# Token halves as slot groups, and expert rows gathered back by token, in a fused mixture-of-experts and attention kernel

## The reference

```
x = x + 0.5 * moe_ffn(layernorm(x))
x = x + attention(layernorm(x))        # 16 heads of 16, rope on q and k, causal softmax
x = x + 0.5 * moe_ffn(layernorm(x))

moe_ffn(x): probs = softmax(x @ gate_w.T)             # 8 experts
            top_w, sel = top_k(probs, 2); top_w /= sum(top_w)
            per expert e: (silu(x @ w_gate[e]) * (x @ w_up[e])) @ w_down[e]     # F = 176
            weighted sum of the two chosen experts' outputs
```

## Time and profile before

| | us |
|---|---|
| median of 3 runs (1216.02 to 1219.74) | 1216.24 |
| the profiled execution's own time | 1216.84 |
| its span, first to last instruction | 1215.1 |
| busy PE, DVE, ACT, POOL | 1002.9, 846.8, 630.8, 588.9 |

### The profile page before, as it was taken

The page is one execution under the profiler, slowest core; times in us unless marked ns, Lnnn a source line. Parts: engine busy times, 40 slices in busy tenths (PEclk is TensorE's granted clock), DMA queues, the critical chain, the costliest instruction groups (busy, mean ns, idle before and its releaser), DMA issues. The chain is left out here.

```text
span 1215.1 us, 24056 instructions
## 1 busy us (share of the span) xinstructions
PE 1002.9 (83%) x6998; PEld 644.2 (53%) x6998; DVE 846.8 (70%) x2632; ACT 630.8 (52%) x1318; POOL 588.9 (48%) x756
## 2 busy tenths in 40 slices
PE   1649998974888489999999999999988569998850
PEld 1438997863767223333333333333347349998750
DVE  5585444435999498999989998988529684443347
ACT  1504554444777216666666666666774505554430
POOL 2937777765999302222222222222239127777740
PEclk9857999996999659999999999999989858999985
DMA  6803333325565511111111111110022413333349
GB/s 212 278 12 102 105 102 104 105 92 158 155 180 164 161 61 47 57 56 60 59 57 57 56 60 55 55 54 2 2 75 71 140 31 105 104 103 104 104 149 338
DMA packets 84524, 121.19 MB, mean 100 GB/s; under 512 B 10920, under 2 KB 63920, under 8 KB 81200
## 3 DMA queue, kind: packets, MB, share of 16 engines
q1 hardware_dynamic: 63424, 75.08, 19.8%
q0 software_dynamic: 13632, 37.24, 9.7%
q10 hardware_dynamic: 7344, 7.34, 1.8%
HBM read 75.51 MB, written 43.78 MB: 98 GB/s over the span
## 5 line engine op out<-in xcount | busy, mean ns | idle before, releaser
L1352 ACT ACTIVATE a_probs<-a_ps_s 128x1024 f32<-128x1024 f32 (+3 forms) x384 | 294.2, 813 | 172.8 <-PE a_ps_s L1384 171.6
L1267 POOL TENSOR_SCALAR_AFFINE_SELECT a_probs<-a_probs 128x256 f32<-128x256 f32 x256 | 102.9, 408 | 368.9 <-ACT a_probs L1352 366.2
L1285 DVE CUSTOM_DVE_ANT_0 a_unused<-a_ps_m,const_sb 128x128 bf16<-128x128 f32 (+3 forms) x512 | 234.1, 485 | 26.6 <-PE a_ps_m L1369 16.7
L1369 PE MATMUL a_ps_m<-st_k,st_q 96*128 96x512 bf16 (+3 forms) x768 | 219.6, 344 | 22.3 <-PEq L167 14.9
L378 POOL DMA_INDIRECT v_sb<-xn_dram,f_token_i x142 | 139.7, 984 | 104.7 <-DVE f_token_i L486 62.0
L1287 DVE TENSOR_REDUCE a_max_a<-a_ps_m 128x1 f32<-128x512 f32 x256 | 175.7, 686 | 13.9 <-PE a_ps_m L1369 13.7
L1384 PE MATMUL a_ps_s<-st_q,st_k 98*128 98x512 bf16 (+3 forms) x768 | 180.6, 329 | 1.5 <-ACT a_probs L1352 1.4
L532 DVE TENSOR_TENSOR f_h<-f_ps_gu,f_sg 128x176 f32<-128x176 f32 x142 | 48.5, 341 | 185.2 <-ACT f_sg L598 185.1
L1369 PEld LDWEIGHTS a_ps_m<-st_k,st_q 96*128 96x128 bf16 x768 | 67.8, 98 | 194.3 <-DVE a_max_a L1287 55.2
L1397 PE MATMUL a_ps_ctx<-a_probs,a_v_st 128*32 128x512 f32 (+3 forms) x1536 | 163.6, 498 | 1.3 <-POOL a_probs L1267 0.7
L382 POOL DMA_INDIRECT y_dram<-v_sb,f_pair_i x142 | 140.0, 986 | 44.0 <-issue 38.1
(11 more groups left out here) (193 smaller groups left out, 2018.8 us busy)
## 6 DMA issues: line engine op xcount, KB each, us to landing
xn_dram<-v_sb SPq DMA_DIRECT2D x64, 128.0 KB, 3.7
v_sb<-y_dram SPq DMA_DIRECT2D x32, 256.0 KB, 5.5
st_q<-qk_dram SPq DMA_DIRECT2D x16, 384.0 KB
st_k<-qk_dram SPq DMA_DIRECT2D x16, 384.0 KB
st_q<-y_dram SPq DMA_DIRECT2D x16, 256.0 KB, 3.3
st_k<-y_dram SPq DMA_DIRECT2D x16, 256.0 KB, 3.2
qk_dram<-st_rT_hi SPq DMA_DIRECT2D x16, 256.0 KB, 3.0
qk_dram<-st_rT_mid SPq DMA_DIRECT2D x16, 256.0 KB, 3.5
```

The source lines that it names most:

```text
L1267: pool.affine_select(out=tri, in_=tri, compare_op=ALU.is_ge, fill=zero, base=0, pattern=[[0, 2], [1, P]], channel_multiplier=-1).then_inc( ...
L1285: dve.tensor_tensor_reduce(unused[:, bank, 0:nk], ps, cst("mask")[:, HALF - nk:HALF], 1.0, NEG, ALU.add, ALU.max, at).then_inc(taken, 1)
L1352: act.activation(probs[:, s % 4, :, 0:nq], ps_s[s % 2][:, :, 0:nq], ACT.Exp, scale=float(HD) ** -0.5).then_inc(exp_done, 1)
L1369: pe.matmul(ps_m[bank][:, 0:nk], q_st[b][0:MAX_ROW, h, P * i:P * i + P], k_st[b][0:MAX_ROW, h, k0:k0 + nk], start=True, stop=True).then_in ...
```

## The change

Slots are grouped by token half first and by expert within it: the first 39 slot tiles (CT = 32 + 7) hold pairs of the first 16 token tiles only, the other 39 those of the last 16. That makes 78 slot tiles instead of 71. One scan over 256 values takes the place of eight, with a correction at the edge of each of 16 groups (edge, shift). Owners are found in three passes over (slot tiles, lots): (0 to 16, lots 0 and 2), (16 to 39, lots 0 and 2), (39 to 78, lots 1 and 3), 96 matmuls instead of 128; pair_i and the treatment of empty slots are gone.

The results are no longer scattered. SP stores each slot tile linearly to y_dram, and GpSimd gathers 128 rows of 1 KB back by token, one indirect transfer for each token tile and choice (gather_y, with the rows' numbers kept in y_rows). The 32 gathers of the first half run beside the experts of the second half, one a step from step 43 on, and VectorE mixes them into x_sb three steps behind (mix); in f1 VectorE takes the statistics of these 16 tiles in the same steps and GpSimd raises the 16 variances to the power at the end, in f2 SP issues four of the eight output stores in these steps. The 32 gathers of the second half come behind the experts: in f2 right away, in f1 within the projection (four gathers in five steps, GATHERS), where ScalarE now weighs both results and GpSimd adds both; VectorE's mix_second is gone. The sum of the rope's two products moves from GpSimd to VectorE for the first 22 tiles (LATE) and stays on GpSimd for the last ten.

```diff
-SLOT_TILES = TOPK * NT + E - 1
+HALVES = 2
+HT = NT // HALVES
+CT = TOPK * HT + E - 1
+SLOT_TILES = HALVES * CT
+ROWS_OF_HALF = TOPK * HT
...
+YB = 8
+Y_LAG = 4
+MIX_LAG = 3
...
+def token_row(m):
+
+    return 2 * (m // 4) + m % 2, m // 2 % 2
+
+
+def rows_mixed(t):
+
+    return 4 * (t // 2) + t % 2 + 3
...
+        OUT_AT = [CT + Y_LAG + MIX_LAG + 8 * (q + 1) - 1 for q in range(HT // 4 - 1)] + [SLOT_TILES - 1]
+
+        def store_out(eng, q):
+
+            eng.wait_ge(mixed, 8 * (q + 1))
+            eng.dma_start(out[q * 4 * P:(q + 1) * 4 * P, :].rearrange("(t p) d -> p t d", p=P), x_sb[:, 4 * q:4 * q + 4, :]).then_inc(out_stored, 16)
...
+            for j in range(SLOT_TILES):
+                sp.wait_ge(y_out, j + 1)
+                sp.dma_start(y_dram[j * P:(j + 1) * P, :], y_sb[:, j % DEEP, :]).then_inc(stored[j % DEEP], 16)
+                if out is not None and j in OUT_AT:
+                    store_out(sp, OUT_AT.index(j))
             for q in range(DEEP):
-                sp.wait_ge(scattered[q], 16 * len(range(q, SLOT_TILES, DEEP)))
+                sp.wait_ge(stored[q], 16 * len(range(q, SLOT_TILES, DEEP)))
             if out is not None:
-                for t in range(NT):
-                    sp.wait_ge(mixed, t - 7 + 8)
-                    sp.dma_start(yb[:, t % 8, :, :].rearrange("p c d -> p (c d)"),
-                                 y_dram[t * P * TOPK:(t + 1) * P * TOPK, :].rearrange("(p c) d -> p (c d)", c=TOPK)
-                                 ).then_inc(y_in[t % 8], 16)
...
-            def scatter(j, slot, pair):
-                pool.wait_ge(y_out, j + 1)
-                pool.indirect_dma_start(y_dram, bass.IndirectOffsetOnAxis(ap=pair, axis=0), y_sb[:, slot, :], None).then_inc(scattered[slot], 16)
-
-            def step(j, u, token, pair):
-
-                if token is not None:
-                    if j + XDEEP + 1 == FIRST:
-                        pool.wait_ge(slots_ready, 2)
+            def gather_y(m):
+                t, c = token_row(m)
+                wait(pool, mixed, m - YB + 1)
+                row = y_rows[:, c * NT + t:c * NT + t + 1]
+                pool.indirect_dma_start(yg[:, m % YB, :], None, y_dram[0:CT * P, :] if m < ROWS_OF_HALF else y_dram, bass.IndirectOffsetOnAxis(ap=row, axis=0)).then_inc(y_in[m % YB], 16)
+
+            def wait_stored(tiles):
+                for q in range(DEEP):
+                    pool.wait_ge(stored[q], 16 * len(range(q, tiles, DEEP)))
+
+            for j in range(-XDEEP - 1, SLOT_TILES + 2):
+                ahead = j + XDEEP + 1
+                if is_tile(ahead):
+                    if ahead in (FIRST, CT):
+                        pool.wait_ge(slots_ready, 2 if ahead == FIRST else 3)
                     wait(pool, xT_ready, j + 2)
-                    gather((j + XDEEP + 1) % XDEEP, token)
-                if pair is not None:
-                    scatter(j - 2, (j - 2) % DEEP, pair)
-
-            def fixed_step(j):
-                step(j, j % 4, token_i[:, j + XDEEP + 1:j + XDEEP + 2] if is_tile(j + XDEEP + 1) else None, pair_i[:, j - 2:j - 1] if is_tile(j - 2) else None)
-
-            for j in range(-XDEEP - 1, SLOT_TILES + 2):
-                fixed_step(j)
+                    gather(ahead % XDEEP, token_i[:, ahead:ahead + 1])
+                if j == CT + Y_LAG:
+                    wait_stored(CT)
+                if 0 <= j - CT - Y_LAG < ROWS_OF_HALF:
+                    gather_y(j - CT - Y_LAG)
+            if out is not None:
+                wait_stored(SLOT_TILES)
+                for m in range(ROWS_OF_HALF, TOPK * NT):
+                    gather_y(m)
+            else:
+                norm = Own(pool, norm_own)
+                norm.then_wait(pool.memset(minus_half[:], -0.5))
+                pool.wait_ge(var_ready, HT // 4)
+                norm.then_wait(pool.tensor_tensor(rstd[:, 0:HT], rstd[:, 0:HT], minus_half[:], ALU.pow))
+                norm.then_wait(pool.tensor_tensor(nmr[:, 0:HT], nmr[:, 0:HT], rstd[:, 0:HT], ALU.mult))
...
+            by_group = [P, GROUPS, HT]
+            base_by_group = base[:].rearrange("p (g t) -> p g t", t=HT)
...
+            for half in range(HALVES):
+                of = slice(E * half, E * (half + 1))
+                own.inc(dve.tensor_tensor_scan(last_tile[:, of], ones_bf[:, 0:E], n_tiles[:, of], float(CT * half), ALU.mult, ALU.add))
             own.wait()
...
-            def tile_hits(at, lot, j0, j1, ready):
-
-                n, of = j1 - j0, slice(LOT * lot, LOT * (lot + 1))
+            def row_hits(lot):
+
+                own.inc(dve.tensor_tensor(at_row[:, lot, :, :], count_lot[:], slot_p[:, LOT * lot:LOT * (lot + 1)].unsqueeze(1).to_broadcast([P, P, LOT]),
+                                          ALU.is_equal))
+
+            def tile_hits(i, lot):
+
+                j0, j1, lots = PASSES[i]
+                at, n, of = at_tile[i][:, lots.index(lot), :, :], j1 - j0, slice(LOT * lot, LOT * (lot + 1))
                 hit, by_tile_no, per_tile = at[:, n:2 * n, :], at[:, 0:n, :], [P, n, LOT]
                 own.then_wait(dve.tensor_tensor(hit, count_lot[:, j0:j1, :], slot_j[:, of].unsqueeze(1).to_broadcast(per_tile), ALU.is_equal))
-                own.then_wait(dve.tensor_tensor(by_tile_no, hit, tile256[:, of].unsqueeze(1).to_broadcast(per_tile), ALU.mult))
-                dve.tensor_scalar(hit, hit, cst("low")[:, LOT * lot // NT:LOT * lot // NT + 1], None, ALU.mult).then_inc(ready, 1)
...
+                own.then_wait(dve.tensor_tensor(by_tile_no, hit, tile128[:, of].unsqueeze(1).to_broadcast(per_tile), ALU.mult))
+                dve.tensor_scalar(hit, hit, cst("low"), None, ALU.mult).then_inc(one_hot_ready, 1)
+
+            def owners(i):
+
+                j0, j1, _ = PASSES[i]
+                ps, n, of = ps_owner[i], j1 - j0, slice(j0, j1)
+                dve.wait_ge(owned, i + 1)
+                own.then_wait(dve.tensor_scalar(low[:, of], ps[:, n:2 * n], -1.0, None, ALU.add))
+                own.then_wait(dve.tensor_tensor(token_up[:, of], ps[:, 0:n], low[:, of], ALU.add))
+                dve.tensor_scalar(token_i[:, of], token_up[:, of], T - 1, None, ALU.bitwise_and).then_inc(slots_ready, 1)
+
+            for lot in LOTS_OF[0]:
+                row_hits(lot)
+                tile_hits(0, lot)
+            for lot in LOTS_OF[0]:
+                tile_hits(1, lot)
+            owners(0)
+            for lot in LOTS_OF[1]:
+                row_hits(lot)
+                tile_hits(2, lot)
...
-            later_hits(2)
-            later_hits(3)
+            owners(1)
...
-            dve.wait_ge(later_owned, 1)
-            owners(ps_later, FIRST, SLOT_TILES)
+            owners(2)
...
+            def mix(m):
+                t, c = token_row(m)
+                dve.wait_ge(y_in[m % YB], 16 * (m // YB + 1))
+                if c:
+                    dve.wait_ge(mixed, m - 1)
+                dve.scalar_tensor_tensor(x_sb[:, t, :], yg[:, m % YB, :], w_mix[:, c, t:t + 1], x_sb[:, t, :], ALU.mult, ALU.add).then_inc(mixed, 1)
+
+            moments_of = Moments(dve, stats_own, stats, mv, x_sb, rstd, nmr)
+
+            def moments_after(m):
+
+                for t in range(HT):
+                    if rows_mixed(t) + 1 == m:
+                        dve.wait_ge(mixed, rows_mixed(t))
+                        moments_of.tile(t, t % 8)
+                    if rows_mixed(t) + 2 == m and t % 4 == 3:
+                        moments_of.four(t // 4, var_ready)
...
+                if 0 <= j - CT - Y_LAG - MIX_LAG < ROWS_OF_HALF:
+                    mix(j - CT - Y_LAG - MIX_LAG)
+                if out is None:
+                    moments_after(j - CT - Y_LAG - MIX_LAG)
...
-            def mix(t, u, c):
-                dve.scalar_tensor_tensor(x_sb[:, t, :], yb[:, u, c, :], w_mix[:, c, bass.ds(t, 1)], x_sb[:, t, :],
-                                         ALU.mult, ALU.add).then_inc(mixed if c else mix_own, 1)
...
             if out is not None:
-                for t in range(NT):
-                    mix_step(t, t % 8)
-                dve.wait_ge(mix_own, NT)
-                mix(NT - 1, 7, 1)
+                for m in range(ROWS_OF_HALF, TOPK * NT):
+                    mix(m)
+            else:
+                for m in range(SLOT_TILES + 2 - CT - Y_LAG - MIX_LAG, ROWS_OF_HALF + 4):
+                    moments_after(m)
...
-                wait(act, scattered[u], 16 * (j // DEEP))
+                wait(act, stored[u], 16 * (j // DEEP))
...
-            for i in range(TOPK * NT):
-                lot = i // LOT
-                pe.wait_ge(first_hot_ready, lot + 1)
-                mm = pe.matmul(ps_first, at_row[:, lot, :, i % LOT], at_first[:, lot, :, i % LOT], start=(i == 0), stop=(i == TOPK * NT - 1))
-            mm.then_inc(first_owned, 1)
-            for i in range(TOPK * NT):
-                lot = i // LOT
-                pe.wait_ge(later_hot_ready, lot + 1)
```

(76 more changed lines are left out.)

213 lines of the change are left out of this document (98 added, 115 removed).

## The result

The changed kernel took 1238.99 us (median of 4 runs, 1235.87 to 1241.44) where the kernel before, measured beside it, took 1216.77 (1216.02 to 1219.74). The ratio is 1.0177, interval 1.0146 to 1.0207: 1.8% slower. I had forecast 1211.6, with a range from 1206 to 1223.

What follows compares the result with a forecast made beforehand. Bounds by stage: VectorE in routing, TensorE then GpSimd in experts, VectorE and GpSimd in projection. Through hand-over -4.0, projection -5.8, tail +5.2: -4.6 from 1216.84 gives 1212.2, less 0.6 is 1211.6 us; range 1206 to 1223.

Steps and rivals of the forecast that it cites:

- Routing: In each FFN, up to the first gate_up: VectorE's shorter list lets gate_up of tile 0 start 5.9 us earlier.
- Experts: Both FFNs: TensorE's 2.13 us a tile holds for all 78 tiles; last y_copy at 264.0 (f1) and 1169.3 (f2).
- rival D: Experts: first-half gathers not hidden, GpSimd falls behind and VectorE waits for y rows; +10, 1222 us; chance 0.10.
- Tail: Second FFN, last y_copy to the end: store landing, 31 gather periods, landing, mix, end; 50.95 us, +5.2 in the sum.
- Rival B: Tail and projection: each gather is held by a mix, locked in step; at a 1.50 us period 1224.2 us; chance 0.11.
- G: Period of one GpSimd row gather in projection and tail, taken as 1.30 us; 0.63 us in all for each 0.01.
- 4.0 of barrier: First FFN's hand-over: after about 3.4 us behind y_copy, a barrier of 4.0 us, so the projection starts at 271.4.
- I price a sum at 1.0: Projection: each of 22 rope sums moved to VectorE costs 1.0 us, leaving its list level with GpSimd's.
- what ends is GpSimd's list: Projection: GpSimd's work up to tile 22's rope sum sets the path; tile 24's rope at +97.7, was +103.5; -5.8 us.
- Rival C: Projection: VectorE's rope sums take 1.4 us, its list 9 us longer than GpSimd's; 1220.6 us in all; chance 0.11.
- Rival A: Projection and tail: nothing contends, gather period 1.27 us, rope sums 0.69 us; 1206.7 us in all; chance 0.14.
- the 2.6 us that I took for a row gather: Landing time of a row gather, put at 2.6 us in experts and tail.

Runs made afterwards that it cites:

- run of the second FFN alone: The kernel before with the changed FFN in its second place only, first FFN and projection as before: 1223.59 us, ratio 1.0048.
- early drain: The changed kernel with one GpSimd drain added behind the last row gather of the first FFN's first half: 1228.09 us, ratio 1.0087.
- distance run: The changed kernel with gathered rows in the projection weighed four steps behind their gather instead of two, added five instead of three: 1233.25 us, ratio 1.0118.
- run with all mends: The changed kernel with early drain, rope sums reading PSUM, rows weighed and added two steps later, and a drain ahead of f2's tail: 1210.12 us, ratio 0.9928.

## Why the prediction failed, step by step

**Routing** was right twice: -6.1 and -5.8 for -5.9. **Experts** were right to 1.1 us (f1) and 0.2 (f2); rival D, the first half not hidden, is excluded. Its sign, VectorE waiting for y rows inside the experts, is there (6.6 us in f1, 6.9 in f2), but in the steps from 43 to 60 TensorE's tiles are 2.13 and 2.16 us apart. **Tail**: 50.48 for 50.95, by nearly the same terms (2.8 for the store, 31 x 1.25, 2.8 for the last landing, 0.5 for the mix, 5.6 to the end). Rival B, the lockstep with the mix, is excluded there: G is 1.25. The run of the second FFN alone shows that its +5 stands by itself.

**Hand-over: the step "4.0 of barrier" failed.** The 3.4 ahead of it was right (264.91 to 268.11 is 3.2). The 4.01 of the earlier trace rows is the price of a barrier behind a stage in which GpSimd had issued no indirect transfer. Behind f1 its drain ran 9.04 us. In the kernel before the same drain ran beside the landing of the last scatters and ended 3.2 us behind it, and I priced that whole stretch as a landing. So I took away a wait that wasn't the last one; I had not asked what else stood in those 8.7 us. What follows GpSimd's last work is 10.9 us (9.24 of drain, 1.66 to the first instruction) where I had put 4.0. The early drain shows it: 5.39 instead of 14.10.

**Projection: the step "I price a sum at 1.0" failed**, and with it the path, "what ends is GpSimd's list". The mean over all 22 sums is 1.62. At 0.62 more each, 22 sums are 13.6 us on VectorE, and it is VectorE that tile 24 hangs on: GpSimd's sums of tiles 22 and 23 wait for VectorE's products (1.57 and 1.10 us), the other way round than I had it. GpSimd's list grew by less: G is 1.34 over all 32 gathers (1.16 busy, 0.18 issue) for the forecast 1.30, and not the 1.40 and more behind rival B, since the first nine run ahead of the first sum; an add is 0.86 for 0.76. That is some 4 us together. Beside the held sums VectorE stands idle for 12.7 us between 340 and tile 24, 9.3 of them in the two waits behind late rows shown above. By these numbers the two are more than the 19.8 us that tile 24 is late (+117.5 for +97.7), so at 1.0 a sum VectorE's list was some 6 us shorter than GpSimd's and not level with it; that is an estimate from the terms named here. The evidence was in the rows that I quoted: VectorE's mix at 0.76 instead of 0.44, that is, held for part of each GpSimd instruction. I used it to weigh G and not for the new sum, which reads SBUF twice just as the mix did. And I bounded the sum by one GpSimd add; it can be caught by r_low (1.16) or by two instructions in a row (2.44 at 334.93). The base was off as well: 1.08 at the least, where I took the 0.69 of the earlier trace rows. That row is a product that writes its result in plain order; the rope sum writes its result with a step of four elements. Whether this is the reason, no run shows. Rival C, a sum of 1.4, was right in kind, with a chance of 0.11. It gave 1220.6 and fell short because it left GpSimd at full pace, and knew nothing of the drain and the late rows. Rival A, nothing contends, is excluded by the same rows.

The Trainium skill, SBUF — State Buffer, section "SBUF: two separate sides", calls the interface that VectorE and GpSimd share an exclusive lock, held for the whole instruction, which a VectorE instruction with two SBUF inputs contends for with a GpSimd instruction that reads SBUF. The trace agrees: 0.96 and 0.95 from r_low's end to the sum's end in the timeline above, 0.71 twice from the sum's end to the gather's. Which part of a gather is held, no run here shows. The same page of the Trainium skill, section "Who interferes with whom", says that a VectorE instruction with at most one SBUF input stays out of it, the performance modes aside; 1.10 for 1.63 with one operand in PSUM agrees.

**Landing: the 2.6 us that I took for a row gather** held in the tail (2.8) and not in the projection (up to 10.2 beside SyncE's loads). The distance of two steps between gather and weighing was not examined as a wait at all, though the prediction did so for the three steps in the experts: what was queued behind it was x_high, and with it the next tile. The distance run is worth 0.59%, some 7 us.

**How the miss adds up.** The hand-over's 6.7 is the drain. Of the projection's 21.3, the run with all mends gives back 20.0 (157.59 to 137.63), against 136.3 forecast: with the three costs gone the number that I had summed is right to 1.3 us. In part that is luck. It is one profile of each, the length of one projection is uncertain by about 6 us, and the path is another than I summed: from tile 0's rope to tile 24's VectorE is busy 81.5 of 85.7 us in that run, GpSimd 75.9. That kernel's ratio is 0.9928; the forecast of 1211.6 on 1216.24 would be 0.9962.

## What to carry to other kernels

Before pricing a removed wait, list what else runs inside the same stretch (drains, sequencer instructions, other landings): the longest of these, and not zero, is what remains. Work moved to VectorE beside a busy GpSimd is priced by how many of its operands lie in SBUF: in this case, with two, count its own time plus the rest of GpSimd's running instruction, and charge GpSimd for the time too; with one left in PSUM, count neither. A consumer that waits for a gather in an engine's queue needs the distance of the longest landing beside the largest neighbouring transfer, not of the median.

## What the runs showed of the hardware that was not expected

- GpSimd's drain runs on after its last work when indirect transfers came since the last drain: 9.24 us beyond it after 110 (first FFN, changed; 9.05 in the early drain), 2.70 after 32 (the projection; 3.14 in the tail of the kernel with all mends), 0.07 after none. The number of transfers isn't all that sets it: after 142 it is 6.36 (changed second FFN, 1224.07 + 14.04 - 1231.75) and, with half of them scatters, 4.98 (first FFN, before). What does is open. At the kernel's end it costs 0.8 us, since the last stores land beside it.
- A drain issued early runs about as long (9.05 us beyond the last gather), and the next one is then short (0.05).
- A gather of 128 rows lands after 2.7 us at the least, and after up to 10.2 beside a 384 KB load.
